# Routing of the second image started ahead of the expert tiles, with 79 tiles, ten output buffers and a later second product

## What is computed

```python
x = x + conv_ref(ln_c(x), ...)             # 4 dilated branches, projection, group norm, relu
t = to_tokens(x)                           # 9216 tokens per image, 256 wide
t = t + moe(ln_t(t), router_w, w1, b1, w2, b2)
...
logits = tokens @ router_w.T               # moe: 8 experts, 2 for each token
rw, re = top_k(softmax(logits), 2)
out = tokens
for e in range(8):
    h = gelu(tokens @ w1[e] + b1[e])
    y = h @ w2[e] + b2[e]
    out = out + combine[:, e:e + 1] * y
```

## Time and profile before

| | us |
|---|---|
| median of 3 runs | 2252.12 |
| lowest, highest | 2251.94, 2254.53 |
| the profiled execution | 2248.74 |
| its span, first to last instruction | 2246.9 |
| busy PE | 1910.4 (85%) |
| busy DVE | 1560.9 (69%) |
| busy ACT | 1333.7 (59%) |
| busy POOL | 1083.1 (48%) |

### The profile page before, as it was taken

How to read it: one execution, slowest core, us unless ns; L and a number is a source line. 1 busy time by engine, 2 the same in 40 slices (tenths; PEclk the granted TensorE clock), 3 DMA queues, 4 the chain that set the end, 5 groups by cost and what they waited for, 6 DMA issues and landing times.

```text
span 2246.9 us, 56560 instructions
## 1 busy us (share of the span) xinstructions
PE 1910.4 (85%) x20204; PEld 1832.1 (82%) x20204; DVE 1560.9 (69%) x4184; ACT 1333.7 (59%) x2877; POOL 1083.1 (48%) x1430
## 2 busy tenths in 40 slices
PE   5899799999969997999998895888888868999943
PEld 4899798999859997898888884888887768999932
DVE  4577675666556775777777774688887856777765
ACT  4677343333327774556556541887777758888822
POOL 3666212222215663145655562367777775555510
PEclk9999799999979998999999997898899989999965
DMA  4332597567554434677888879567667667888889
GB/s 143 105 106 78 145 294 189 141 173 174 153 142 133 132 102 111 190 228 216 227 232 245 237 209 322 171 219 227 224 218 225 202 192 274 284 282 283 280 310 368
DMA packets 341802, 459.87 MB, mean 205 GB/s; under 512 B 82677, under 2 KB 262709, under 8 KB 339173
## 3 DMA queue, kind: packets, MB, share of 16 engines
q1 hardware_dynamic: 231208, 246.52, 38.7%
q10 hardware_dynamic: 68433, 109.55, 14.9%
q0 software_dynamic: 41888, 100.18, 13.0%
HBM read 291.86 MB, written 174.69 MB: 208 GB/s over the span
## 4 chain that ended last, share of the span: by engine, by line
PE 46%; ACT 14%; DVE 13%; POOL 9%; issue 7%; DMA 7%; ACTq 3%; SPq 1%; POOLq 1%; DVEq 1%
PE ps_y L424 17%; PE ps_a L424 7%; PE ps_o L1050 6%; PE ps_b L987 4%; POOL expert_in L2148 4%; PE ps L424 3%; ACT w_now L1494 3%; POOL expert_out L2224 3%; ACT e_act L1483 3%; DMA o_acc<-res_scratch 3%; PE ps_tok L897 1%; DVE cat_lo L1938 1%; PE ps_o L1037 1%; ACT h_hi L1486 1%; DMA y_scratch<-y_acc 1%
## 5 line engine op out<-in xcount | busy, mean ns | idle before, releaser
L424 PE MATMUL ps_y<-cat_hi,wp 128*128 128x288 f32 x2048 | 483.5, 312 | 1.8 <-DVE cat_lo L1938 1.8
L2224 POOL DMA_INDIRECT expert_out<-e_out,e_dest x320 | 327.4, 1023 | 248.2 <-DVE e_out L2048 177.2
L2202 POOL DMA_DIRECT2D patches<-rows_scratch x340 | 190.4, 604 | 499.3 <-PE ps_o L1037 301.4
L424 PEld LDWEIGHTS ps_y<-cat_hi,wp 128*128 128x128 f32 x2048 | 354.4, 195 | 2.0 <-DVE cat_lo L1938 2.0
L2148 POOL DMA_INDIRECT expert_in<-r_ln,r_pos x288 | 290.0, 1007 | 106.3 <-issue 86.3
L2168 POOL TENSOR_TENSOR taps<-taps,g_rows 96x108 f32<-96x108 f32 (+2 forms) x416 | 243.8, 611 | 162.5 <-ACT g_rows L1310 158.6
L1379 ACT ACTIVATE bands<-ps_b 112x288 f16<-112x288 f32 (+4 forms) x256 | 105.1, 411 | 345.4 <-PE ps_b L987 331.9
L424 PE MATMUL ps_y<-cat_lo,wp 128*128 128x288 f32 x1024 | 308.1, 301 | 0.0
L424 PE MATMUL ps<-w,h_hi 128*128 x1280 | 258.5, 301 | 53.9 <-DVE h_lo L2037 51.1
L1938 DVE SCALAR_TENSOR_TENSOR cat_lo<-ps_o,cat_hi 128x288 fp32r<-128x288 f32 (+1 forms) x576 | 228.2, 419 | 92.9 <-ACT cat_hi L1385 89.4
L424 PE MATMUL ps<-e_hi,w_now 128*128 128x256 f32 x1280 | 266.1, 292 | 4.8 <-ACT w_now L1494 2.1
(11 more groups left out here) (201 smaller groups left out, 4488.3 us busy)
## 6 DMA issues: line engine op xcount, KB each, us to landing
e_x<-expert_in SPq DMA_DIRECT2D x160, 260.0 KB
patches<-rows_scratch SPq DMA_DIRECT2D x160, 192.0 KB
patches<-rows_scratch SPq DMA_DIRECT2D x256, 108.0 KB
patches<-rows_scratch SPq DMA_DIRECT2D x204, 112.0 KB
x_in<-in_x SPq DMA_DIRECT2D x48, 384.0 KB, 3.7
rows_scratch<-rows_st SPq DMA_DIRECT2D x48, 384.0 KB, 4.2
r_x<-in_x ACTq DMA_DIRECT2D x72, 256.0 KB
r_y<-y_scratch ACTq DMA_DIRECT2D x72, 256.0 KB
```

The lines of the kernel that those rows point to most:

```text
L424: mm = eng.matmul(out, lhs[p], rhs[q], start=start and n == 0, stop=stop and n == 2)
L2202: pool.dma_start(patch_target(s, n), patch_source(m, s, n)).then_inc(patch_pooled[s % RING], 16)
L2224: pool.indirect_dma_start(out=ys_dram, out_offset=bass.IndirectOffsetOnAxis(ap=e_dest[:, i, j:j + 1], axis=0), in_=e_out[:, u, j], in_offs ...
```

## The change

- The expert loop has 79 tiles for each image instead of 80 (tables keep their 80 places).
- Routing of image 1: six slots are done before the first expert tile (`AHEAD`, 24 ticks), and then one slot for each step. The group factors, the first blocks and their scaling move in front of the loop too, and the load of the second weights `w2` moves behind the loads of the first two blocks. The rank comes two slots after a pair's end, not four.
- The routing products have two PSUM banks `ps_r`, used in turn, instead of `ps_k` alone; the logits of odd and even tiles lie in different banks and are kept with two copies.
- The second product, and with it the bias and the send, comes two steps after the first product instead of one; h has three buffers.
- Outputs have ten buffers (`e_out` and six more, `e_more`, in the room of the early residuals) up to tile 140, then four. POOL waits itself for the scatter four tiles before.
- `scatter_after` is moved up by up to four tiles for the later pairs.
- Image 0's output groups stand in steps 93 to 154, one every 2.65 steps; there are four early residuals instead of five.

```diff
-ETILES = PIX * TOP // S + E
+ETABLE = PIX * TOP // S + E
+ETILES = ETABLE - 1
...
-EARLY = 5
+EARLY = 4
+BEHIND = 2
+HB = 3
...
+EO_MORE = 6
...
-        h_hi = sbuf(ctx, "h_hi", [128, 2, CC, S], F32R)
-        h_lo = sbuf(ctx, "h_lo", [128, 2, CC, S], F32R)
+        h_hi = sbuf(ctx, "h_hi", [128, HB, CC, S], F32R)
+        h_lo = sbuf(ctx, "h_lo", [128, HB, CC, S], F32R)
...
+        with ExitStack() as r1:
+            e_more = sbuf(r1, "e_more", [128, EO_MORE, S // 128, C])
         res_early = sbuf(ctx, "res_early", [128, EARLY, TT, C])
...
+                ps_r = psum(r2, "ps_r", [128, 2, 512])
...
-        RANK_AT = TP + 4
-        SLOTS = RANK_AT + TP * (CPAIRS - 1) + 1
+        RANK_AT = (TP + 4, TP + 2)
+        SLOTS = [at_ + TP * (CPAIRS - 1) + 1 for at_ in RANK_AT]
+        AHEAD = 24
...
-        expert_ticks = [4 * 3 + (7 * k_ + 1) // 2 for k_ in range(SLOTS)]
+        expert_ticks = [4 * k_ - AHEAD for k_ in range(SLOTS[1])]
...
-        OUT_FIRST = ETILES + 7
+        OUT_RING = EO + EO_MORE
+        SHORT = (STREAM - 2 * EARLY - 4) // OUT_RING * OUT_RING
+
+        def out_buffer(n):
+
+            u = n % OUT_RING if n < SHORT else (n - SHORT) % EO
+            return e_out[:, u] if u < EO else e_more[:, u - EO]
+
+        def out_user_before(n):
+
+            return n - OUT_RING if n < SHORT + EO else n - EO
+
+        def sent_through(n):
+
+            return 16 * (S // 128) * (n // EO + 1)
+
+        OUT_FIRST = ETILES + 14
+        OUT_LAST = STREAM - 4
+        out_tile = {OUT_FIRST + g_ * (OUT_LAST - OUT_FIRST) // (GROUPS_OUT - 1): g_ for g_ in range(GROUPS_OUT)}
...
             def turn_tile(t):
 
                 j, k = divmod(t, BT)
+                bank, raw = (ps_k, t % TP) if t < ITILES else (ps_r[:, t % 2], t % TP // 2)
...
-                    after(pe, r_kept, slots_before(r, k))
+                    after(pe, r_kept, slots_before(r, max(k - 1, 0) if r else k))
...
+            pe.wait_ge(r_kept, slots_before(1, 0))
+            group_sums(1, ps_g)
             turn_in(0)
             turn_in(1)
+            for u in range(-AHEAD, 0):
+                routing(1, u)
             pe.wait_ge(y_added, 4 * IMAGES * Y_UNITS)
...
-                if n:
-                    second_product(n - 1)
+                if n >= BEHIND:
+                    second_product(n - BEHIND)
...
                 act.wait_ge(e_first, n + 1)
+                after(act, h_lo_done, n - 1)
...
-            act.wait_ge(tabled, TABLE_ALL)
-            input_hi(0)
-            input_hi(1)
-            act.wait_ge(w_loaded_1, 32)
-            weights_hi(0)
-            weights_hi(1)
+            group_deviation(1)
             act.wait_ge(y_stored, 16 * (24 + 18))
             act.wait_ge(y_pooled, 16 * 6)
             for j in range(RY):
                 load_block(BLOCKS + j)
+            act.dma_start(w2[:].rearrange("p e z c -> p (e z c)").bitcast(F32), w_dram[1].rearrange("p e z c -> p (e z c)")).then_inc(w_loaded_2, 16)
+            act.wait_ge(tabled, TABLE_ALL)
+            input_hi(0)
+            input_hi(1)
+            act.wait_ge(gn_dve, 18)
+            for j in range(RY):
+                relu_block(BLOCKS + j)
+            load_block(BLOCKS + RY)
+            for u in range(-AHEAD, 0):
+                routing(1, u)
+            act.wait_ge(w_loaded_1, 32)
+            weights_hi(0)
+            weights_hi(1)
...
+                used = out_user_before(n)
+                if used >= 0:
+                    dve.wait_ge(e_scattered[used % EO], sent_through(used))
...
-                if n:
-                    output(n - 1)
+                if n >= BEHIND:
+                    output(n - BEHIND)
...
+                if n >= EO:
+                    pool.wait_ge(e_scattered[u], sent_through(n - EO))
                 pool.wait_ge(e_out_done, n + 1)
...
-                return plans[1].placed(p) // 4 - 1 + q
+                return plans[1].placed(p) // 4 - BEHIND + q - (OUT_RING - EO - 1) * p // CPAIRS
```

More of the change, by code:

```diff
@@ L348, in build @@
             with ExitStack() as r2:
-                psum(r2, "routing", [128, 512])
+                ps_r = psum(r2, "ps_r", [128, 2, 512])
+            with ExitStack() as r2:
+                psum(r2, "first_routing", [128, 512])
                 ps_g = psum(r2, "ps_g", [128, 2, 256])
@@ L529, in __init__ @@
                 self.pair_end = {self.ticks[TP * p + TP - 1]: p for p in range(CPAIRS)}
-                self.pair_rank = {self.ticks[TP * p + RANK_AT]: p for p in range(CPAIRS)}
+                self.pair_rank = {self.ticks[TP * p + rank_at]: p for p in range(CPAIRS)}
             def kept(self, p, h):
@@ L818, in _ @@
                 if n == STREAM - 2 * EARLY:
+                    for u in range(EO):
+                        sp.wait_ge(e_scattered[u], sent_all(u, SHORT))
                     for u in range(2):
@@ L1230, in keep_slot @@
                         act.wait_ge(r_scattered[p % HELD], 16 * TP * TOP * (p // HELD))
-                    last = act.activation(r_ln[:, p % HELD, k % TP, 0:C], ps_k[:, 0:C], ACT.Copy)
-                    if k % TP == TP - 1:
+                    bank = ps_r[:, k % 2] if r else ps_k
+                    last = act.activation(r_ln[:, p % HELD, k % TP, 0:C], bank[:, 0:C], ACT.Copy)
+                    if r and k % TP >= TP - 2:
+                        after(act, r_read, p - 1)
+                        odd = r_raw[:, p % 2].rearrange("p (k b e) -> p k b e", b=2, e=E)[:, :, k % 2]
+                        last = act.activation(odd, bank[:, 256:256 + TP // 2 * E].rearrange("p (k e) -> p k e", e=E), ACT.Copy)
+                    elif not r and k % TP == TP - 1:
                         after(act, r_read, p - 1)
                         last = act.activation(r_raw[:, p % 2], ps_k[:, 256:256 + TP * E], ACT.Copy)
-                ranked = ranked_in(k)
+                ranked = ranked_in(r, k)
                 if ranked is not None:
@@ L1572, in _ @@
                     write_out(g)
-                if n >= OUT_FIRST - 3 and sent < GROUPS_OUT and sent <= (n - OUT_FIRST + 3) // 3 + OB - 2:
+                begun = sum(n_ <= n + 3 for n_ in out_tile)
+                if n >= OUT_FIRST - 3 and sent < GROUPS_OUT and sent <= begun + OB - 3:
                     load_outputs(sent)
@@ L2020, in _ @@
             dve.drain()
+            group_factors(1, ps_g)
             def input_lo(n):
@@ L2101, in _ @@
             dve.memset(r_ln[:, 1, :, MARK:XC], 0.0)
-            group_factors(1, ps_g)
+            for j in range(RY):
+                add_block(BLOCKS + j)
+            for u in range(-AHEAD, 0):
+                routing(1, u)
             for n in range(STREAM):
                 hidden_lo(n)
-                if n == 2:
-                    add_block(BLOCKS)
-                    add_block(BLOCKS + 1)
                 routing(1, 4 * n)
@@ L2125, in _ @@
                     weigh_second(g)
-            output(STREAM - 1)
+            for n in range(STREAM - BEHIND, STREAM):
+                output(n)
             for g in range(GROUPS_OUT, 2 * GROUPS_OUT):
```

110 lines of the change are left out of this document (50 added, 60 removed).

## The result

| | kernel before | changed kernel |
|---|---|---|
| median, 20 runs each on one chip | 2251.19 us | 2257.24 us |
| lowest, highest | 2240.59, 2256.63 | 2243.40, 2269.17 |
| profiled execution, its span | 2248.74, 2246.9 | 2252.9, 2251.0 |
| mean granted clock of TensorE | 0.923 | 0.913 |

The ratio is **1.0036, 95% interval 1.0023 to 1.0049: slower**, by little but clear of 1, where 2236 us, 0.7% faster, was forecast.

A forecast was written before the change was run, and what follows sets the result against it. POOL was taken to bound the second stretch from 1477 us on; gate -17, 79 tiles and outputs 0, tail +1 gave -16 us on 2252, so 2236 us, with its own range 2230 to 2243 and a full range of 2218 to 2256.

The forecast's parts named there:

- POOL bounds the second stretch: Image 0's experts beside image 1's routing: POOL is the bound from 1477 us on, at 1.315 us for each DMA.
- rival 4: POOL's DMAs stretch because DVE is fuller, the excess over 1.27 us doubling: +12 us, 2248; 7%.
- POOL's start: First product to POOL's first send: 20 us against 16.3 before, start at 1451; bounds 15 to 25.
- rival 2: In the passage, the second weights don't hold up the third block: first product at 1421, 2226 us; 13%.
- 2 for gaps: POOL's work to the gate: 276 DMAs at 1.315 us, 363 us, plus 2 us for gaps in the first steps.
- the others run ahead by some 0.4 us a step: Second stretch: other engines outpace POOL's 5.26 us a step, so sends lag by up to 7 tiles, held by ten buffers.
- They must reach step 69 before POOL wants it: Feeding POOL: the other engines must get to step 69, where the last pair is placed, before POOL wants it.
- rival 1: DVE sets the pace: at 5.6 us a step, gate 1845 and 2260 us, slower; against the forecast from 5.25; 12%.
- SP issues the eight fills: Fills of the regions' ends follow tile 78's load; POOL's some 20 DMAs, 26 us, before the gate hide them.
- 79 tiles and outputs: After the gate: 22.6 us off the ACT-bound part, 22.9 us for 7 more tiles alone; zero, bounds -4 and +4.
- rival 3: Output loads come late in the third stretch, DVE waiting 0.8 us per group: +19 us, 2255; 8%.
- Tail: DMA-bound last outputs: one more residual, 384 KB at 393 GB/s, +1.0 us.

The follow-up runs named there:

- c3_more: Changed kernel with rank four slots behind, routing slots back, groups every third step, plus w2 loaded behind the third block and fills ahead of tiles 76 to 78: 2244.61 us, 0.9983.
- c4_passage: Changed kernel with rank four slots behind, routing slots back, groups every third step, and the passage put back as in the kernel before: 2244.71 us, 0.9989.
- c5_behind1: c4_passage with the second product one step behind the first, as before, instead of two: 2242.91 us, 0.9976.

## Why the prediction was wrong

**POOL bounds the second stretch, 1.315 us for each DMA: right.** In the executions at 0.92 the time from first send to the start of the last routing scatter is the number of DMAs times 1.31 to 1.33 and the gaps over 0.9 us: 276 and 13.8 us with the change (373), 288 and 26.8 in the second trace of before (406), 278 and 27.0 with ticks and groups back (391). The sends did run ahead of what four buffers hold: up to nine outputs stood finished and unsent (at tile 66), forecast seven, where before it was four. DVE was fuller (269.6 us of 323, 83.5%, against 287.1 of 355, 80.9%) and POOL's DMAs no slower, mean 1.008 us against 1.019 and 1.037: rival 4 fell. That a fuller DVE stretches them was my guess, and no run shows it.

**"POOL's start", 20 us from first product to first send: 24.5.** I let the added DVE work and the saved group sums cancel. They don't: PE waits for r_either at the first pair, and dense routing slots from step 0 fill the first steps. Without slots in them it is 14.0 us. 4.5 us of the 24. The first product itself came 2 us earlier than forecast, and the third block was scaled at 1413.9 after 7.40 us of waiting, forecast 1417.5: rival 2 has no support, since moving w2 brought nothing.

**"2 for gaps": 12.** This is the step that failed first, and with it "the others run ahead by some 0.4 us a step". "They must reach step 69 before POOL wants it" was taken as a question of mean pace, 4.96 us against 5.26, and 4.96 was read from tiles 3 to 12 of before. Those nine steps hold the choices of one pair (its r_either at step 9); later a pair comes every 5 or 6 steps. Over the same nine steps the changed kernel with the rank at four slots takes 4.76 us a step, what I forecast, and from tile 9 to 69 it takes 5.10: the sample was too light, by 0.3 us a step (0.1 of it is DVE waiting for a free output buffer, 7.5 us in all). On top comes the rank product at two slots, which I named only in rival 1, where it was to need 5.25 us a step to matter. It cost PE 50.7 us, the pace became 5.22, and POOL stood three times before a scatter that was placed as early as before but whose rows were late. Putting the rank back takes the gaps away and adds four DMAs, so that 276 DMAs with 2 us of gaps were not to be had either way. Rival 1 happened in its mild form, which I had priced at nothing: short of the threshold in the mean, past it in single steps.

**"SP issues the eight fills ... POOL has then some 20 DMAs, 26 us, before the gate, which hide them": no.** The fills hang on tile 78's load, at 1814 us, and the last scatter came only 9.6 us later. +3.4 us. The cover was worked out from a tile chain 0.4 us a step ahead; at 5.22 there were 6 DMAs left. In the run with rank at four slots the 3.4 us are gone without touching the fills; the fills alone were tried only at 0.85, where other waits open the gate.

**"79 tiles and outputs: zero, bounds -4 and +4": +8.3.** The sum of ACT's time was right as far as it went (the steps beside a group still take 11 us for three). Left out were two things: the loads, now bunched two steps apart, that let tile loads land late (3.7 us of waiting with even spacing, 13.1 without), which is rival 3 at another place than I put it (PE's turn-in, not DVE), with the lower clock behind them (0.97 over 1880 to 2130, 1.00 before); and the drain, +3.3 us, since with the second product two steps back the last three outputs come at once and POOL sends them at 1.28 us a DMA. The drain is there in every trace with two steps at 0.92 (9.1 to 9.7 us). Of the first term the size is uncertain: with the same spacing the third stretch took 311.1, 319.4 and 323.0 us in three kernels, with one, three and four long steps, and 311.1 is what the kernel before takes.

**Tail, +1.0: +1.5.** Right.

**What became of each part of the change** at 0.92, by the runs: fewer tiles -0.13% (interval to 0); rank at two slots +0.32%, by the difference of two ratios; routing slots ahead of the loop about +0.26%; the close groups 0.19 to 0.26%. Each ratio has an interval of 0.13 to 0.2% to either side, so that differences of 0.26% stand at the edge of what they tell, and only the rank's is clear. Ten buffers, the earlier scatters, the two banks, the new passage and the second product's second step are what is left, and with them and 79 tiles the kernel stands at 0.9959: a gate 13 us or more earlier than before by the convolution's end (445.6 against 458.3 to 461.4), of which 10 DMAs fewer ahead of the last scatter are 13. Its three neighbours with the same buffers and scatters, c3_more, c4_passage and c5_behind1, have the gate at 452.2 to 454.2 and ratios of 0.9976 to 0.9989, so 0.1 to 0.4% faster is what these runs bear out. That the buffers are the cause is argued from the unsent outputs, not shown: no run took them away alone.

## What to carry to other kernels

When a change moves a wait earlier in an in-order queue (here a product that reads another engine's work), cost the wait itself at its new place, in the worst step and not in the mean of all, and ask what stands behind it. Read a pace only from steps that carry the steady load: nine steps with one pair's choices gave 4.96 us, sixty with ten pairs 5.10 and more. When a bound engine is relieved by 10%, look for the next chain within 10%: here the tile chain, SP's fills behind it and PE's late loads took the gain back. And measure the same edit at both mean clocks: it cost 0.3% at 0.92, where POOL was the bound, and 2% at 0.86, where it was not.

## What the hardware showed that was not expected

The same program took 2249 us in some sets and 2524 to 2551 in others. The difference begins after 800 us: up to there both show 0.96 to 0.97, in the second stretch 0.89 against 0.74, means over two levels, 1.00 and 0.50: read in windows of 1 us, the traces of the kernel before, of the changed kernel in its first execution and of the changed kernel in the second set show 0.50 in 304, 345 and 696 windows and 1.00 in 1872, 1825 and 1785, and nowhere two neighbouring windows between the two. PE had been 92% busy in 400 to 800 in both. At the lower mean PE also stands idle with no releaser, waits in 1700 to 2100:

```profile
PE ps L432 <- issue: 73.0, 92, 3.0
```

Some 65 of these 73 us lie in the long steps shown in the second set: 32 products in 20 us at a granted level of 0.50 that gave 28 in 5.8 us in the first execution. So the granted clock alone doesn't tell how fast PE goes. It isn't shown that the chip decides, either: the last two sets are recorded on a chip of the same number, the first at 0.92 and 2249 us, the second at 0.86 and 2548.

The kernel uses one core, and no run here shows what the other cores of its chip did: what brings a set into one or the other stays open.
